# Mask reads ahead of the values' store, the third patch behind the first, eight experts behind the second store

## The reference, cut to what matters

```python
x = x + einsum('bct,bcd->bdt', x, W0[cond])                    # layer 0
x = x + x @ W1.T + ((x @ A[adp].T) @ B[adp].T) * s[adp]        # layer 1
q, k, v = x @ Wq.T, x @ Wk.T, x @ Wv.T                         # layer 2; q, k: rms norm, then rope
pos = kv_lens[:, None] + arange(T)
k_blocks = k_blocks.at[blk, :, pos % 16, :].set(k)             # blk = block_tables[pos // 16]
v_blocks = v_blocks.at[blk, :, pos % 16, :].set(v)
allowed = (kpos <= pos) & (kpos > pos - 128)
x = x + softmax(where(allowed, q @ k_all.T / 16, -inf)) @ v_all @ Wo.T
x = x + einsum('bsi,bio->bso', x, W3[ids]) + b3[ids]           # layer 3
```

## Time and profile before

| what | value |
|---|---|
| time, median of 3 runs | 160.92 us (160.25 to 162.71) |
| the profiled execution's own time | 162.41 us |
| its span | 160.6 us |
| TensorE busy, weight load busy | 119.0 us (74%), 92.3 us (57%) |
| VectorE, ScalarE, GpSimd busy | 97.1, 80.1, 63.4 us |
| DMA | 34.19 MB, mean 213 GB/s |
| mean granted clock of TensorE | 0.87 of 2.4 GHz |

### The profile page before, as it was taken

One profiled execution on the slowest core, in us unless ns is written; L12 is line 12 of the kernel. 1 busy time (PEld: TensorE's weight loads), 2 busy tenths in 40 slices (PEclk: granted clock), 3 DMA queues, 4 the chain that ended last, 5 costly groups with the idle time before them and its releaser, 6 DMA issues.

```text
span 160.6 us, 4138 instructions
## 1 busy us (share of the span) xinstructions
PE 119.0 (74%) x1418; PEld 92.3 (57%) x1418; DVE 97.1 (60%) x318; ACT 80.1 (50%) x233; POOL 63.4 (39%) x65
## 2 busy tenths in 40 slices
PE   7669999989989486683599820497006999999762
PEld 7558858888465176462478520295005777867641
DVE  0599868477998822599519900740018769899361
ACT  3124295665233639977159720436004567888300
POOL 6677605704784500053605610262004756454000
PEclk9956999999999999789569995569755599999999
DMA  3985999989983374649875588733987888862100
GB/s 102 223 268 156 348 422 365 292 314 402 389 268 124 92 241 141 174 107 293 249 243 146 158 234 224 215 75 86 270 267 218 242 248 266 271 183 97 37 33 33
DMA packets 34333, 34.19 MB, mean 213 GB/s; under 512 B 9482, under 2 KB 32398, under 8 KB 33055
## 3 DMA queue, kind: packets, MB, share of 16 engines
q1 hardware_dynamic: 31369, 20.57, 45.7%
q0 software_dynamic: 2528, 12.82, 21.7%
q10 hardware_dynamic: 416, 0.56, 1.1%
HBM read 31.39 MB, written 6.64 MB: 237 GB/s over the span
## 4 chain that ended last, share of the span: by engine, by line
SPq 25%; PE 25%; DMA 17%; issue 13%; DVE 9%; POOL 4%; ACT 3%; another core or an unknown queue 2%; POOLq 1%; DVEq 0%
DMA v_rows<-blkp 7%; SPq L370 6%; SPq L369 5%; DMA blkp<-wr_rows,patch_i 4%; SPq L410 4%; POOL wr_rows L514 3%; SPq L389 3%; PE bank L1137 3%; SPq L390 3%; PE bank L1148 3%; PE bank L996 3%; DMA lens_i<-in_itok_B 3%; SPq L409 2%; PE bank L1003 2%; PE bank L1163 2%
## 5 line engine op out<-in xcount | busy, mean ns | idle before, releaser
L537 POOL TENSOR_TENSOR xin_m<-xin_m,ri 128x704 f32<-128x704 f32 x15 | 22.0, 1465 | 45.7 <-DVE ri L945 45.6
L689 ACT ACTIVATE xin_m<-kvn_m,nb 128x176 f32<-128x176 f32 x64 | 27.5, 438 | 18.2 <-DVE nb L932 18.2
L1083 PE MATMUL bank<-kt_m,natQ 32*64 32x176 f32 x256 | 15.6, 365 | 22.3 <-DVE nb L932 20.6
L975 DVE TENSOR_TENSOR blkp<-blkp,cst 128x512 f32<-128x512 f32 x16 | 14.9, 971 | 27.1 <-DMA blkp<-in_L_cond_W 27.1
L1083 PEld LDWEIGHTS bank<-kt_m,natQ 32*64 32x64 f32 x256 | 9.6, 153 | 26.5 <-issue 25.6
L932 DVE CUSTOM_DVE_ANT_0 kvn_m<-bank,mask_m 128x176 f32<-128x176 f32 x64 | 18.0, 336 | 7.7 <-PE bank L1083 6.3
L699 ACT COPY x_m<-bank 128x512 f32<-128x512 f32 x16 | 9.4, 585 | 15.0 <-PE bank L1095 12.5
L514 POOL DMA_INDIRECT wr_rows<-kvn_m,row_i x8 | 10.6, 1321 | 8.0 <-DVEq L888 5.9
L689 ACT ACTIVATION_READ_ACCUMULATOR xin_m<-kvn_m,nb 128x1 f32 x64 | 12.4, 194 | 0.0
L1095 PE MATMUL bank<-cst,xin_m 128*128 128x128 f32 x64 | 11.4, 307 | 0.7 <-POOL xin_m L537 0.7
L1137 PE MATMUL bank<-w_m,WoT 128*128 128x128 f32 x64 | 11.0, 324 | 1.0 <-DVE w_m L964 0.9
(11 more groups left out here) (194 smaller groups left out, 267.2 us busy)
## 6 DMA issues: line engine op xcount, KB each, us to landing
blkp<-in_L_cond_W SPq DMA_DIRECT2D x32, 256.0 KB, 3.6
v_rows<-blkp SPq DMA_DIRECT2D x2, 968.0 KB
wr_rows<-blkp SPq DMA_DIRECT2D x1, 1536.0 KB, 8.2
mask_m<-mask_rows SPq DMA_DIRECT2D x32, 44.0 KB
vm_m<-v_rows SPq DMA_DIRECT2D x4, 320.0 KB, 3.9
xin_m<-in_x SPq DMA_DIRECT2D x2, 512.0 KB
out<-wq_m SPq DMA_DIRECT2D x8, 128.0 KB, 2.5
v_rows<-blkp SPq DMA_DIRECT2D x1, 880.0 KB
```

The source lines that it names most:

```text
L537: pool.tensor_tensor(e_, e_, ri[:, p % 2, :].unsqueeze(2).broadcast_to([P, 4, KEYS]), ALU.mult).then_inc(s_pn, 1)
L689: act.activation(pr_seq(n % 2, u, j), S[:, n % 2, u, j, :], ACT.Exp, bias=nb[:, n % 2, 2 * u + j:2 * u + j + 1], scale=-1.0, accum_out=rs[ ...
L975: tt(w_, w_, ident.unsqueeze(1).broadcast_to([P, B4, P]), ALU.add).then_inc(s_wx, 1)
L1083: i_ = mm(bank[2 + (2 * p + u) % 3][GS * T * k:GS * T * k + GS * T, j * KEYS:(j + 1) * KEYS], QT[h, b // B4, b % B4, :], KT[h, b, :], star ...
```

## The change

Six mask reads go ahead of the writer blocks' store, the other 26 right behind it. Behind them SyncE's order is: store 0, read 0, store 1, experts 0 to 7, read 1, store 2, experts 8 to 15, read 2. Patch 2 waits for patch 0 instead of store 0. Stores 1 and 2 write the whole tile, keys and values, 128 partitions of 16 KB, into a new tensor `kv_rows`; the reads take the values out of it. Store 0 stays as it was.

```diff
@@ -114,7 +114,8 @@
     with ctx:
         wr_rows = nc.dram_tensor("wr_rows", [ROWS, 2 * KV], F32).ap()
         wr_blocks = wr_rows.rearrange("(p o) c -> p (o c)", o=BLOCK)
-        v_rows = nc.dram_tensor("v_rows", [NU, P, BLOCK, KV], F32).ap()
+        v_rows = nc.dram_tensor("v_rows", [P, BLOCK, KV], F32).ap()
+        kv_rows = nc.dram_tensor("kv_rows", [NU - 1, P, BLOCK * 2 * KV], F32).ap()
         mask_rows = nc.dram_tensor("mask_rows", [P, KEYS + LAST], BF16).ap()

         cst = sb("cst", [P, cols.width])
@@ -369,11 +370,13 @@
                 x = sp.value_load(shift_i[0:1, b:b + 1], min_val=0, max_val=LAST)
                 sp.dma_start(mask[:, b, :], mask_rows[:, bass.ds(x, KEYS)]).then_inc(s_mask[b // MB], 16)

+            for b in range(6):
+                load_mask(b)

             for kv in range(2):
                 sp.wait_ge(s_perm[NU, kv], 1)
             sp.dma_start(wr_blocks, blkw[0:NWI, :]).then_inc(s_base, 16)
-            for b in range(2 * MB):
+            for b in range(6, B):
                 load_mask(b)
             sp.wait_ge(s_ids, 16)

@@ -393,7 +396,10 @@

             def values_out(u):
                 sp.wait_ge(s_patch[u], 16)
-                sp.dma_start(v_rows[u, 0:PU[u]], by_o[u][0:PU[u], :, 1, :]).then_inc(s_vo[u], 16)
+                if u == 0:
+                    sp.dma_start(v_rows[0:PU[u]], by_o[u][0:PU[u], :, 1, :]).then_inc(s_vo[u], 16)
+                else:
+                    sp.dma_start(kv_rows[u - 1], blkp[u][:, :]).then_inc(s_vo[u], 16)

             def values_back(u):
                 sp.wait_ge(s_vo[u], 16)
@@ -402,7 +408,10 @@
                     for i in ((0, 0), (0, 1)):
                         sp.wait_ge(s_perm[i], 1)
                 b0, b1 = SEQS[0] * u, SEQS[0] * u + SEQS[u]
-                src = v_rows[u, 0:PU[u]].rearrange("(b j) o c -> (j o) b c", j=WB)
+                if u == 0:
+                    src = v_rows[0:PU[u]].rearrange("(b j) o c -> (j o) b c", j=WB)
+                else:
+                    src = kv_rows[u - 1][0:PU[u], :].rearrange("(b j) (o k c) -> (j o) b k c", j=WB, o=BLOCK, k=2)[:, :, 1, :]
                 for i in range(2):
                     b = b0 + (b0 + i) % 2
                     main, tail, lo = (KB, 0, KB) if i else (0, P, 0)
@@ -410,23 +419,15 @@
                     sp.dma_start(Vt[lo:lo + KB, b // 2:(b1 - 1 - i) // 2 + 1, i, :], src[tail:tail + KB, b - b0::2, :]).then_inc(s_v[u], 16)

             values_out(0)
-            for b in range(2 * MB, 2 * MB + 4):
-                load_mask(b)
             values_back(0)
-            for b in range(4):
+            values_out(1)
+            for b in range(8):
                 expert(b)
-            values_out(1)
-            for b in range(2 * MB + 4, 3 * MB):
-                load_mask(b)
             values_back(1)
-            for b in range(4, 8):
-                expert(b)
             values_out(2)
-            for b in range(3 * MB, B):
-                load_mask(b)
-            values_back(2)
             for b in range(8, NE):
                 expert(b)
+            values_back(2)
             nxt = NE
             for g in range(NT):
                 while nxt < B and (nxt - NE) // B4 <= g - 1:
@@ -527,7 +528,7 @@
             patch(0)
             patch(1)

-            pool.wait_ge(s_vo[0], 16)
+            pool.wait_ge(s_patch[0], 16)
             patch(2)
             pool.wait_ge(s_eidi, 1)
             pool.wait_ge(s_l1, 4)
```

## The result

The changed kernel takes 146.18 us (median of three, 145.9 to 146.58) against 160.92: a ratio of 0.911, with an interval of 0.904 to 0.917, so 8 to 10% faster. Some executions of a kernel take over 1.5% longer than its fastest, whatever the change; the ratios leave them out, the medians do not. The profiled execution took 146.18 us with a span of 144.4, against 162.41 and 160.6.

The account below looks back on a forecast made before the run. Everything up to group 2 was taken as paced by expert landings behind SyncE's queue. Group 2 at 107.4 instead of 119.98 gains 12.6 us, the 40.6 behind it stay: 149.8 profiled, median 148.3, range 141 to 154.

Parts of the forecast that it names:

- Masks: SyncE's mask loads moved ahead: 26 end at about 59.5 to 61.4, pushing the first store 0 to 1.8 us, 0.3 taken.
- the sum: Queue times added from store 1's issue at 74.7 through stores, reads and experts: group 0 at 88.5, group 2 at 107.4.
- Third patch: Issued near 60.3 instead of 69.06, landing near 70; TensorE's 4.6 us wait goes, gaining nothing by itself.
- What the store loses the read gains: The third patch runs beside store 0 instead of the first read of the values; net effect taken as zero.
- the bad end of 2.8: The third patch's estimated 0.8 MB at most, all lost in the store of v_rows: 2.8 us later.
- First store and read: Masks between them gain nothing; the third patch's wait goes, so store 1 leaves at 74.7 instead of 78.91, gaining 4.2 us.
- The store holds the experts: Experts 0 to 3 queue behind store 1, not beside it: group 0 released at 88.5, 4.9 us later than before.
- Size of the store: Each whole-row store, 2.10 MB: 7.4 us at 284 GB/s, with 4.9 at 424 GB/s and 10.9 as alternatives.
- The tail: Everything behind group 2's release, 40.6 us, which the change was to leave untouched.
- The rival in which group 4 waits for its experts: Read of unit 2 delays experts 16 to 19 to 121 to 124; 2 to 5 us return, 150 to 153; chance 0.20.
- Signs: What the new profile would show if right: mask and patch times, group times, group 2's wait, two store stretches.
- Slower: Rival with whole rows written slowly: break-even at 13.7 us per store, 3.2 us slower at 15.3; chance 0.07, half slower.

Follow-up runs that it names:

- the run with masks between: The changed kernel with the last 16 mask reads put back between the steps, 4, 4 and 8 behind stores 0, 1 and 2: 155.57 us, ratio 0.967.
- the run with the patch early alone: The kernel before, with only the third patch moved up to wait for the first patch instead of store 0: 158.86 us, ratio 1.001.
- The run with store 1 early: The changed kernel with store 1 issued right behind store 0, ahead of the first read: 142.11 us, ratio 0.889.
- the run with four experts first: The changed kernel with experts 0 to 3 issued ahead of store 1, as in the kernel before: 150.72 us, ratio 0.938.

## Why the prediction was right, point by point

Between the profiled executions 12.6 us were forecast and 16.2 measured: 15.4 up to group 2 and 0.8 behind it. The mechanism was as forecast; the difference is in the size of terms. That group 0 and store 1 came so near their forecasts is in part luck, as errors cancelled.

- *Masks.* Six went ahead of the writer blocks' store, which left at 26.54 against 26.46, and 26 behind it took 31.63 us, 1.22 each. Store 0 left at 59.80. The push, 0.3 in the sum, was nothing here. (The lower bound in the prediction is 27.87 + 20.6 + 10.6 = 59.1, not 59.5; both lie before 59.99.) That the four masks behind store 0 were free was borne out by the run with masks between; what the masks as a whole are worth depends on the order around them, 1.9% in the kernel before and 6% in the changed one.
- *Third patch.* Its stall went, and "buys nothing by itself" held in the run with the patch early alone. "What the store loses the read gains" was wrong in the second half: the store lost 4.3 us or more (by the trace's events it had landed at 68.30 in the kernel before, so 8.3 us and not 9.1), beyond the bad end of 2.8, and it was store 1 and not the read that gained. The net of zero held, for another reason than the one given.
- *First store and read.* Store 1 was to leave at 74.7 and left at 75.32. Two errors cancel in that, by luck: the store lasted 4.3 us longer, and the read's issues took 2.1 us instead of 4.7 (the last was not held for 3.20).
- *The store holds the experts.* Forecast for group 0: 88.5; measured: 89.28. The run with store 1 early and the order of the packets confirm the mechanism.
- *Size of the store.* 7.4 us, taken from the writer blocks' 284 GB/s, was too long: 2.10 MB at 412 GB/s are 5.1 us. The low end of 4.9 us was the true one. This is the term that was mis-sized, by 2.3 us for each of two stores. At group 0 it did not show. The store's packets start at 78.26, where the sum has 77.4, as the data of the first read still ran; and the experts' last packet ended at 86.91, 2.4 us before VectorE started, a time to landing for which the sum has no term. The experts' own rate was low, too: the 282 GB/s were read from a stretch in which a good part of the third read ran.
- *Group 1* was to come at 96.9 without a wait, and came at 97.84 without one. *Group 2* was to come at 107.4, 4.5 us after VectorE asked; it came at 104.62, 1.79 after. In the trace store 2's packets start at 93.24, where the sum has 96.3, and store and experts 8 to 11 are through at 102.49, where the sum, with 7.4 and 3.7 us for them, has 107.4. The time to landing, 2.1 us here, takes part of these 4.9 us back. VectorE's own work (97.84 to 102.83) is now nearly as late as the queue.
- *The tail* stood at 39.8 against 40.6. The rival in which group 4 waits for its experts did not come: group 4 started at 116.96 without a wait, 12.3 us behind group 2, where 13.3 were reckoned. In the second execution of the change it did wait, 0.44 us.
- *Signs.* The place of masks and patch and groups 0 and 1 were as named. The stores' two stretches ran at a full DMA share, but for 5 us and at 412 and 432 GB/s, not for 7 us at 285; and the wait at group 2 was 1.79 us, not 3 to 5. Both misses are the mis-sized store.
- *Slower:* the whole rows were fast, 9.8 and 10.2 us to landing, and the point from which that rival decides was 13.7 us of data alone.

## What to carry to other kernels

A store that is read back needs work of the same queue between its issue and its read that lasts as long as its landing (9.8 to 11 us in the change and the run with four experts first); eight 256 KB loads covered it and four did not. But that work stands behind the store's data, so what is needed soonest should not be behind it: issue the store where the queue would wait anyway, as with store 1 behind store 0, which gave 2 to 3% more. Small loads that cost an issuing engine 1 us each are free beside such waits and cost their full time where the queue would otherwise run dry, so the same 16 loads were worth 2% in one order and 6% in another.

## What the runs showed of the hardware that was not expected

- Whole rows of 16 KB were stored at 412 to 432 GB/s with a DMA share of 1.00 to 1.03, where the same kind of store (the writer blocks) had moved at 284 GB/s with a share of 0.95 earlier in the kernel before. A 16 KB packet took some 0.62 us in the fast stores and 0.82 to 0.96 us in the slow one. Why is not shown.
- Loads of 256 KB ran at 355 GB/s when they had piled up in the queue behind a store, at 266 when each was issued as it came, with DMA shares of 1.07 and 0.90.
- A gather of one unit's patches beside a store cost the store 3 to 5 us of landing, with the DMA engines 0.55 to 0.64 busy on the mean. The store spread over 11 or over all 16 engines made no difference to that: one or two engines landed last, up to 4.4 us after 13 of 16 were done. What held these engines was not tried.
